# Spreading a step's four gathers on GpSimd, one step further ahead

## What is computed

```python
# tok: three tables, gathered by token id
item, geo, visit = emb[ids], geo_table[ids], visit_table[ids]     # 64, 64, 24 wide
cat   = concat(gelu(item @ w_item), gelu(geo @ w_geo), gelu(visit @ w_visit))
h     = item + 0.1 * (ids != 0) * (layernorm(gelu(cat @ w_fuse)) * gamma + beta)
# attention, 4 heads of 16, per sequence
x     = layernorm(h);  h = h + softmax(q(x) k(x)^T * scale) v(x) @ Wo
# feed-forward, kept for the 63 tokens of each sequence with the largest x @ wr
x     = layernorm(h);  w = x @ wr
h     = h + x + where(selected, w * (gelu(x @ w1) @ w2), 0)
```

## Time and profile before

| | us |
|---|---|
| median of 3 runs | 517.92 |
| the three runs | 513.45, 517.92, 518.04 |
| the profiled execution, its own time | 516.32 |
| its span, first to last instruction | 514.2 |

### The profile page before, as it was taken

How to read it: one execution, slowest core, us unless ns; L and a number is a source line. 1 busy time by engine, 2 the same in 40 slices (tenths; PEclk the granted TensorE clock), 3 DMA queues, 4 the chain that set the end, 5 groups by cost and what they waited for, 6 DMA issues and landing times. The chain is left out here.

```text
span 514.2 us, 16259 instructions
## 1 busy us (share of the span) xinstructions
PE 456.4 (89%) x5658; PEld 360.1 (70%) x5658; DVE 404.8 (79%) x1656; ACT 373.9 (73%) x662; POOL 343.8 (67%) x412
## 2 busy tenths in 40 slices
PE   4777799999999999999999999999998999788750
PEld 2455677777777777877777778777776877566530
DVE  1466888888888888889888888888886888877397
ACT  1226688888888888888888888888886888665440
POOL 5756677677777777777777767776867777311782
PEclk9899999999999999999999999999998999987755
DMA  4111111211111111111111111111101011000146
GB/s 111 24 26 26 27 27 27 27 26 25 25 25 23 20 22 21 23 20 20 25 25 25 25 25 25 25 25 25 25 14 22 15 24 26 1 4 3 41 122 163
DMA packets 23732, 15.80 MB, mean 31 GB/s; under 512 B 18848, under 2 KB 21536, under 8 KB 23584
## 3 DMA queue, kind: packets, MB, share of 16 engines
q0 software_dynamic: 6144, 9.97, 13.7%
q1 hardware_dynamic: 17568, 5.58, 4.0%
HBM read 11.08 MB, written 4.19 MB: 30 GB/s over the span
## 5 line engine op out<-in xcount | busy, mean ns | idle before, releaser
L312 POOL DMA_INDIRECT G<-table,idx x128 | 126.2, 986 | 62.6 <-issue 54.1
L320 POOL TENSOR_TENSOR rs<-ve,minus_half 128x4 f32<-128x4 f32 x96 | 101.2, 1063 | 28.7 <-DVE ve L660 27.6
L763 DVE TENSOR_REDUCE neg_max<-psum 128x4 f32<-128x512 f32 x128 | 84.4, 680 | 0.9 <-PE psum L1117 0.6
L449 ACT ACTIVATE prob<-psum 128x512 f32<-128x512 f32 x128 | 66.1, 602 | 3.2 <-PE psum L1087 2.9
L1045 PE MATMUL psum<-wt,hid 128*128 128x64 f32 x512 | 66.7, 286 | 1.5 <-ACT hid L456 1.5
L1045 PEld LDWEIGHTS psum<-wt,hid 128*128 128x128 f32 x512 | 63.0, 201 | 2.5 <-ACT hid L456 2.2
L1087 PEld LDWEIGHTS psum<-q_s,k_s 32*128 32x128 f32 x1024 | 32.8, 189 | 20.9 <-DMA q_s<-max_t 11.2
L1087 PE MATMUL psum<-q_s,k_s 32*128 32x128 f32 x1024 | 38.2, 285 | 9.5 <-ACT q_s L523 6.3
L807 DVE TENSOR_SCALAR k_s<-psum,wt 128x512 f32<-128x512 f32 x32 | 24.0, 751 | 28.5 <-PE psum L1198 28.5
L456 ACT ACTIVATE hid<-psum,wt 128x512 f32<-128x512 f32 x64 | 40.5, 683 | 4.8 <-PE psum L1218 2.0
L449 ACT ACT_TABLE_LOAD x31 | 39.8, 1283 | 3.4 <-PE psum L1087 2.9
(11 more groups left out here) (118 smaller groups left out, 1076.7 us busy)
## 6 DMA issues: line engine op xcount, KB each, us to landing
out<-R SPq DMA_DIRECT2D x13, 256.0 KB, 2.6
G<-table,idx POOLq DMA_INDIRECT x128
wt<-packed SPq DMA_DIRECT2D x1, 1028.0 KB, 5.1
q_s<-max_t SPq DMA_DIRECT2D x32, 8.0 KB
out<-R SPq DMA_DIRECT2D x1, 512.0 KB, 3.9
out<-R SPq DMA_DIRECT2D x2, 128.0 KB, 2.9
ids_sb<-ids SPq DMA_DIRECT2D x1, 64.0 KB, 1.8
```

Of the source, the lines that this page charges most:

```text
L312: pool.indirect_dma_start(G[par][:, b, :], None, table, bass.IndirectOffsetOnAxis(ap=idx[par][:, b:b + 1], axis=0),).then_inc(gathered[par ...
L320: pool.tensor_tensor(rs[:, :], ve[:, :], minus_half[:, :], ALU.pow).then_inc(S[dst], 1)
L449: act.activation(prob[:, :, h, :], bank[h].rearrange("p (b q) -> p b q", b=GB), ACT.Exp, scale=SCALE).then_inc(S["prob_ready"], 1)
L763: dve.tensor_reduce(neg_max[:, GB * h:GB * h + GB], bank[h].rearrange("p (b k) -> p b k", b=GB), AX, ALU.max, negate=True).then_inc(S["max ...
```

## The change

GpSimd now gathers group `far` = i+4 in step i. The four gathers of a group are no longer issued together: one stands behind the power for rs3, one behind `add_x3`, and two behind the power for rs1. `visit` and `base` for i+3 come ahead of the power for rs1. There are two buffers for u, so `base` waits for h1_ready of one group earlier. Before the steps GpSimd gathers groups 0, 1 and 2, and group 3 at the end of step -2. VectorE does the fills at its very start, copies gv for groups 0 and 1, and copies indices for i+4. The gathered bytes, the number of gathers and TensorE's and ScalarE's programs stay as they are.

```diff
+            def fetch(g, par, first=0, end=GB):
+
+                if first == 0:
+                    wait(pool, "idx_ready", 1, g, alone=True)
+                    wait(pool, "gt_ready", 1, g - 2, alone=True)
+                    wait(pool, "gv_ready", 1, g - 2, alone=True)
+                    wait(pool, "u_ready", 1, g - 2, alone=True)
+                for b in range(first, end):
...
             def base(g, par):
 
-                wait(pool, "h1_ready", 1, g - 1, alone=True)
+                wait(pool, "h1_ready", 1, g - 2, alone=True)
+                wait(pool, "u_ready", 1, g - 1, alone=True)
...
             fetch(0, 0)
 
-            pool.memset(minus_half[:, :], -0.5)
...
-            visit(0, 0, 0)
+            fetch(1, 1)
             pool.wait_ge(consts_ready, 1)
+            pool.wait_ge(zeros_ready, 3)
+            pool.wait_ge(gathered[0], 64)
             base(0, 0)
+            fetch(2, 0)
...
             def step(i, odd, half):
-                a, d, nxt = i + 2, i - 2, i + 3
+                a, d, nxt, far = i + 2, i - 2, i + 3, i + 4
+                steady = on(far) and not filling(i)
                 if on(d):
                     rstd(ve3, rs3, "ve3_ready", "rs3_ready", d)
-                if on(nxt):
-                    fetch(nxt, 1 - odd)
-                if on(a):
-                    rstd(ve1, rs1, "ve1_ready", "rs1_ready", a)
-                if on(nxt):
-                    visit(nxt, 1 - odd, half + 1 + odd)
+                if steady:
+                    fetch(far, odd, 0, 1)
                 if on(d):
                     weighted(d)
                 if on(d):
                     add_x3(d)
-                if on(nxt):
+                if steady:
+                    fetch(far, odd, 1, 2)
+                if on(nxt) and not (filling(i) and i == -2):
+                    visit(nxt, 1 - odd, half + 1 + odd)
+                if on(nxt) and not filling(i):
                     base(nxt, 1 - odd)
                 if on(a):
+                    rstd(ve1, rs1, "ve1_ready", "rs1_ready", a)
+                if steady:
+                    fetch(far, odd, 2, 3)
+                if steady:
+                    fetch(far, odd, 3, 4)
+                if on(nxt) and filling(i):
+                    base(nxt, 1 - odd)
+                if on(a):
                     rstd(ve2, rs2, "ve2_ready", "rs2_ready", a)
-
-            pipeline(pool, step, ahead=3)
+                if type(i) is int and i == -2:
+                    fetch(3, 1)
+
+            pipeline(pool, step, ahead=4)
...
         def _(dve):
 
+            dve.memset(minus_half[:, :], -0.5)
...
+            for p in range(2):
+                dve.wait_ge(gathered[p], 64)
+                wait(dve, "vt_ready", 1, p - 1)
+                dve.tensor_copy(gv[:, :, :], G[p][:, 0:GB, 2 * D:FEAT]).then_inc(S["gv_ready"], 1)
...
-                if on(i + 3):
-                    next_indices(i + 3, odd)
+                if on(i + 4):
+                    if filling(i):
+                        dve.wait_ge(gathered[odd], 64)
+                    next_indices(i + 4, 1 - odd)
```

More of the change, by code:

```diff
@@ L123, in build @@
         s1 = sb("s1", [P, GB, D])
-        u = sb("u", [P, GB, D])
-        u0 = sb("u0", [P, GB, D])
+        u = [sb(f"u{p}", [P, GB, D]) for p in range(2)]
+        u_base = sb("u_base", [P, GB, D])
         c2 = sb("c2", [P, GB, D])
@@ L239, in filling @@
             return type(i) is int and i < 0
+        def filling(i):
+            return type(i) is int and i < 0
         def ffn_bank(d):
@@ L323, in base @@
             def base(g, par):
-                wait(pool, "h1_ready", 1, g - 1, alone=True)
+                wait(pool, "h1_ready", 1, g - 2, alone=True)
+                wait(pool, "u_ready", 1, g - 1, alone=True)
                 pool.tensor_tensor(
-                    u0[:, :, :], of(valid, g).unsqueeze(2).to_broadcast([P, GB, D]),
+                    u_base[:, :, :], of(valid, g).unsqueeze(2).to_broadcast([P, GB, D]),
                     b_tenth[:, :].unsqueeze(1).to_broadcast([P, GB, D]), ALU.mult
@@ L330, in base @@
                 wait(pool, "u0_ready", 1, g, alone=True)
-                pool.tensor_tensor(u[:, :, :], u0[:, :, :], G[par][:, :, 0:D], ALU.add
+                pool.tensor_tensor(u[par][:, :, :], u_base[:, :, :], G[par][:, :, 0:D], ALU.add
                                    ).then_inc(S["u_ready"], 1)
@@ L612, in _ @@
         def _(dve):
+            dve.memset(minus_half[:, :], -0.5)
+            dve.memset(neg_max[:, :], 0.0)
+            dve.memset(o[:, :, :], 0.0).then_inc(zeros_ready, 1)
+            dve.wait_ge(zeros_ready, 1)
+            dve.memset(o[:, :, D:D + 1], 1.0).then_inc(zeros_ready, 1)
+            for p in range(2):
+                dve.memset(V[p][:, :, :, HD + 1:VC], 0.0)
+                last = dve.memset(V[p][:, :, :, HD:HD + 1], 1.0)
+            last.then_inc(zeros_ready, 1)
             dve.wait_ge(ids_in, 16)
@@ L620, in _ @@
             dve.wait_ge(ids_ready, 2)
-            dve.tensor_copy(idx[0][:, :], of(idx_all, 0)).then_inc(S["idx_ready"], 1)
+            for p in range(2):
+                dve.tensor_copy(idx[p][:, :], of(idx_all, p)).then_inc(S["idx_ready"], 1)
             dve.memset(ones[:, :], 1.0)
@@ L845, in norm1, with rows @@
                 scale(s1, t1, rm1, "s1_ready")
-            def rows(a):
+            def rows(a, odd):
                 wait(dve, "s1_ready", 1, a)
-                dve.tensor_tensor(of(R, a), s1[:, :, :], u[:, :, :], ALU.add
+                dve.tensor_tensor(of(R, a), s1[:, :, :], u[odd][:, :, :], ALU.add
                                   ).then_inc(S["h1_ready"], 1)
@@ L905, in step @@
                 if on(a):
-                    rows(a)
+                    rows(a, odd)
                 if on(e):
@@ L931, in step @@
                     route(d)
-            pipeline(dve, step, ahead=3)
+            pipeline(dve, step, ahead=4)
             take_weights(0)
```

## The result

| us | before | after |
|---|---|---|
| median | 516.25 (4 runs, 513.45 to 518.04) | 523.8 (4 runs, 520.97 to 528.88) |
| the profiled execution, its own time | 516.3 | 521.3 |
| its span | 514.2 | 519.5 |

The ratio is 1.0129, with a 95% interval of 1.0076 to 1.0181. The change made the kernel slower by a little over 1% here. On another chip it came out otherwise; that is told under the experiments, and it matters.

The account below looks back on a forecast made before the run. TensorE bound the kernel at 13.7 us a step, with a GpSimd-VectorE ring of 13.58 only 0.1 under it. 516.3 + 9.4 (loop) + 1.8 (late gather) + 1.0 (start) = 528.5 us; range 511 to 541.

Parts of the forecast that it names:

- slower: Sign of the whole: a time above 523.1 us; chance 0.62.
- ring: Closed loop of GpSimd and VectorE, index copy to next index copy: 13.58 us to grow to 14.2, +9.4 in the loop.
- 14.0 to 14.7 of my forecast: Range of the loop's ring in us under the forecast case, time 523 to 541; chance 0.52.
- no change: Rival: base or the gap before the second gather shorter, ring 13.7 to 13.9 us, time 516 to 519; chance 0.20.
- the start: Steps before the loop: wait for group 1 goes, group 0's power comes late; +1.0 us, between -2.6 and +2.8.
- late gather: Second gather of group 28: the same issue hold of 1.83 us, now on the ring, paid in full: +1.8.
- The ring up to rm: Loop step, from index copy's end through gathers, xw, R, base and power to rm: rm at 7.98 us.
- The 538 us of my estimate: Whole time if base and the power lose one 0.42 us overlap with VectorE per loop step: 24 x 0.42 = 10 us.
- The stretch from rm to the next index copy: Rest of the ring in a loop step, rm's start to the next index copy's end: kept at 6.24 us.
- The first power: Power for rs1 of group 0, at the start: waits behind group 2's gathers, starts at 22.1, 2.8 us late.
- TensorE keeps its own step: Rival: the ring gets shorter, waits on gathers go, loop 327.6 us, whole 509.9; chance 0.18.
- slower still: Rival: three of eight 0.22 us waits on the ring are not hidden, ring 14.9 us, time 545; chance 0.10.

Follow-up runs that it names:

- experiment 1: Changed kernel, with base and the gv copy behind the power for rs1 in the steady steps: 517.0 us, ratio 0.9996 to the kernel before.
- experiment 3: Kernel before, with xw and R moved ahead of the power for rs1: 547.76 us, ratio 1.0629.
- Experiment 4: Changed kernel, with group 2's index copy right behind the first gv copy and three of its gathers ahead of the first power: 519.7 us, ratio 1.0072.
- experiments 1 and 2: For 1 see experiment 1; 2 is the changed kernel with the index copy in the middle of the step before: 520.28 us.
- experiment 7: Changed kernel, with the start's order of Experiment 4 and the index copy in the middle of the step before: 516.74 us, on the third chip 518.53.
- experiment 8: Kernel before, with only the fills and group 0's gv copy moved to VectorE: 568.73 us (ratio 1.012), second run 574.73 (ratio 0.9982).

## Why the prediction was right, and where it was not

The direction and the range held for the pair of kernels it was made for: 523.8 against a forecast of 528.5. The sum was 7.2 us over the profiled execution's 521.3, and its terms were further off than that: they cancelled in part.

That it came out "slower" is in part luck. The measured ring of 13.94 us lies under the 14.0 to 14.7 of my forecast and next to the 13.7 to 13.9 that I had given to "no change". With the loop's measured +3.2 and my own +1.0 and 0 for the rest, the sum is 520.5, within 1%. What carried it over is the start, +4.8 where I had +1.0 and bounds of -2.6 and +2.8. The tail's -2.7, for which I had no term, is mostly the granted clock of that execution.

| step of the sum | predicted | measured |
|---|---|---|
| loop, ring and late gather | +9.4 + 1.8 | +3.2 |
| start | +1.0 | +4.8 |
| tail | 0 | -2.7 |

**The ring up to rm: right, to 0.01 us.** Predicted from the index copy's end: first gather 1.19, xw 2.28, R 2.97, rm 7.98. Measured from 206.95: 1.18, 2.24, 2.92, 7.99. Two sizes within it were off and cancelled: the second gather came 0.16 us behind R, not 0.30, so the power started at 6.52, not 6.74; and it took 1.23 us, not 1.04. So the 0.01 us is luck, the order and the path are not. VectorE's product t (L844), with two SBUF inputs, starts 0.21 us into the second part of `base` on GpSimd, and the power starts 0.48 us into t. t takes 0.80 us in each step of this loop, and 0.42 in experiment 1, where `base` and the power have moved. The SBUF — State Buffer page of the Trainium skill, section "Who interferes with whom", says that a VectorE instruction with two SBUF inputs contends with a GpSimd instruction that reads SBUF; the trace agrees, with 0.38 us lost by t and 0.19 us by the power. The 538 us of my estimate by that page, with 0.42 us lost on the ring in each step, did not come: the ring lost 0.19 at the power.

**The stretch from rm to the next index copy: the mis-sized term.** I took 6.24 us as fixed. It measured 5.95 (214.94 to 220.89), and the ring 13.94, not 14.22. I had named this as a way to be wrong ("if the 6.24 us from rm to the index copy shrank"). In the kernel before, the statistics, ve and the first maximum beside GpSimd's tensor work:

```profile
209.12 1.18 DVE L647 BATCH_NORM_STATS2 st<-R 128x6 f32 x8
...
211.09 0.37 DVE L660 TENSOR_SCALAR ve<-mv 128x4 f32<-128x4 f32 x2
211.41 1.29 DVE L763 TENSOR_REDUCE neg_max<-psum 128x4 f32<-128x512 f32 x2
```

From ve to the maximum this took 0.32 us, and 0.14 after the change; from the statistics to ve it took 1.97, and 1.86 after. GpSimd had copy, xw, R and `base` beside them before, and gathers after. In experiment 3, where xw and R have left this stretch too, it is 5.95 in the step shown; in experiment 1, where the copy and `base` are back in it, 6.40 to 6.44. That their neighbours on GpSimd are the cause fits these four; it was not tried by itself.

**The loop's terms.** My sum meant a loop of 24 x 14.2 + 1.8 = 342.6 us; it took 334.62, 8.0 less. Typical steps took 13.91 (13.89 and 13.93 in turn), which is 7.0 of it. The late gather was held by 1.32 us of issue, not 2.13, and made one long step (15.11, +1.2), which is 0.6. The first two steps (13.67 and 13.75) give 0.4. Against the kernel before, typical steps went from 13.655 (13.61 and 13.70 in turn) to 13.91, times 24 +6.1; but there the late gather had made two long steps (+3.1), which returns 1.9, and the first two steps on either side return another 0.9.

**The start: the mechanism right, the size wrong.** The first power was predicted at 22.1 and came at 22.54, x2 at 27.2 and came at 28.04; TensorE waits at x2, as written. Experiment 4 undoes it and wins 3.6 us. My step failed in the assumption that a gain ahead (TensorE's step starts at 18.36, not 21.02) offsets the delay. TensorE's second step then only waits longer: 3.91 us at x2. Ahead of group 2 that costs 1.8, in the upper part of my bound, and 3.0 more come up to the loop, which I had put at nothing. Of these 1.7 are TensorE's lower granted clock in step 2, which my sum had no term for, and 1.3 stay open.

**The rival that TensorE keeps its own step** has its condition in experiments 1 and 2: with the ring cut, the loop takes 328.1 and 328.7, and I had given it 327.6. The *slower still* rival (eight waits that are not hidden) didn't come: TensorE's and VectorE's waits are explained without it.

**Not foreseen at all:** that the kernel before does not have one speed. My sum is against a profile that shows one chip at one time.

## What to carry to other kernels

When a wait is removed by issuing earlier, look for the closed loop between two engines that the moved work joins: add up both sides of it, from one copy to the next, before counting the idle time as won. Cut the loop where a tiny operation closes it (here a copy of 128x4 indices), and put work that nothing waits for behind the operation that everything waits for. Measure the kernel before and the change on more than one chip, and more than once, before you trust 1%: here the sign hung on it. When an engine shows longer idle time ahead of an operation, measure from its releaser too: here a gather with 2.11 us of idle time was no later behind its index copy than one with 0.93.

## What the runs showed of the chip that I had not expected

- The same kernel took 516 to 517 us in two batches of runs, and 564 and 579 in two others on other chips; the changed kernel took 523.8 and 521.8. Of the kernels run on the latter two, the one of experiment 7 was the fastest there (516.7 and 518.5), on the third 3.3 us under the changed kernel. It was not run on a chip where the kernel before is fast, so that it beats it everywhere is not shown.
- The 114th gather of the program, the second of group 28, is held by 1.3 or 2.1 to 2.2 us of issue in each of the 14 traces, whether it stands in a burst or by itself. After the change:

```profile
378.85 1.00 POOL L317 DMA_INDIRECT G<-table,idx  x1 [1.32 <-issue]
```

  It goes by the place in the program, not by time (378.85 here, 382.44 in the earlier trace rows, 439.0 in the second run of experiment 8).
- The same 762 matmuls of the tail were busy 66.85, 63.81 and 61.74 us at mean granted clocks of 0.76, 0.80 and 0.83: 5 us between kernels whose tails do the same.
